# A gated cross-attention and quantised feed-forward block on one core: preparation and attention merged into one block of instructions, with the gate-weight jobs placed in attention steps

## The reference, cut to what matters

```python
def reference(x, ctx_1024, g_xattn, g_ffn, w_q, w_k, w_v, w_o, w_gate, w_up, w_down):
    # x is (4, 1024, 512), ctx_1024 is (4, 64, 512); 16 heads of 64
    x = x + jnp.tanh(g_xattn[0]) * xattn(_layernorm(x), ctx_1024, ctx_1024, w_q, w_k, w_v, w_o)
    x = x + jnp.tanh(g_ffn[0]) * ffn(_layernorm(x), w_gate, w_up, w_down)
    return x
# xattn: q, k, v projections, scores * 64**-0.5, causal mask (k_pos <= q_pos),
#        softmax over the 64 keys, weights @ v, @ w_o
# ffn:   x = act_qdq(x)                      (quantised by its largest absolute value)
#        up, gate = act_qdq(x @ lpbq_dequant(w_up).T), act_qdq(x @ lpbq_dequant(w_gate).T)
#        gate = act_qdq(gate * fixed_qdq_u16(sigmoid(gate)));  o = act_qdq(gate * up)
#        return o @ lpbq_dequant(w_down).T
# lpbq_dequant: per block of 32 weights, scale = max|w| / 7, round, times scale
```

## Time and profile before

| | us |
|---|---|
| median of 3 runs | 1515.85 (1515.39 to 1516.1) |
| the profiled execution | 1512.33 |
| its span | 1510.5 |
| PE busy | 1331.8 (88%) |
| DVE busy | 1097.1 (73%) |
| ACT busy | 596.8 (40%) |
| POOL busy | 241.3 (16%) |
| first instruction of attention (DVE) | at 71.09 |
| first chunk matmul of attention | at 79.50 |
| first matmul with gate weights (`gate_phase`) | at 586.32 |

### The profile page before, as it was taken

How to read it: one execution, slowest core, us unless ns; L and a number is a source line. 1 busy time by engine, 2 the same in 40 slices (tenths; PEclk the granted TensorE clock), 3 DMA queues, 4 the chain that set the end, 5 groups by cost and what they waited for, 6 DMA issues and landing times. The chain is left out here.

```text
span 1510.5 us, 18719 instructions
## 1 busy us (share of the span) xinstructions
PE 1331.8 (88%) x6141; PEld 1089.7 (72%) x6141; DVE 1097.1 (73%) x1460; ACT 596.8 (40%) x705; POOL 241.3 (16%) x249
## 2 busy tenths in 40 slices
PE   6589999999999985999999989999994009999999
PEld 5468877877886864788888868887883008888887
DVE  5557878878878853667777769998998995455453
ACT  2232232232223212334443335556667973333331
POOL 2112211212212210000100025551101000000000
PEclk9889999999999986999999989999997559999999
DMA  8701211211110117866665689996558863444443
GB/s 290 253 0 36 70 40 53 68 42 49 62 56 35 50 46 300 295 230 236 230 245 191 221 317 309 312 317 214 173 191 322 336 239 120 172 148 167 162 151 118
DMA packets 110998, 259.17 MB, mean 172 GB/s; under 512 B 10848, under 2 KB 23136, under 8 KB 109408
## 3 DMA queue, kind: packets, MB, share of 16 engines
q1 hardware_dynamic: 110656, 258.52, 49.0%
q10 hardware_dynamic: 288, 0.00, 0.0%
HBM read 151.52 MB, written 106.95 MB: 171 GB/s over the span
## 5 line engine op out<-in xcount | busy, mean ns | idle before, releaser
L1065 PE MATMUL gpG<-xph,Wh 128*128 128x512 f32 x384 | 153.1, 399 | 2.0 <-DVE xpl L985 2.0
L1539 PE MATMUL pD<-Wh,xph 128*128 128x512 f32 x384 | 150.3, 391 | 4.6 <-DVE xpl L1518 4.6
L1065 PE MATMUL pU<-xph,Wh 128*128 128x512 f32 x384 | 150.8, 393 | 0.7 <-POOLq L63 0.7
L1065 PE MATMUL gpG<-xph,Wl 128*128 128x512 f32 x384 | 150.7, 393 | 0.0
L1065 PE MATMUL gpG<-xpl,Wh 128*128 128x512 f32 x384 | 150.6, 392 | 0.0
L1065 PE MATMUL pU<-xpl,Wh 128*128 128x512 f32 x384 | 150.5, 392 | 0.0
L1065 PE MATMUL pU<-xph,Wl 128*128 128x512 f32 x384 | 150.3, 392 | 0.0
L1539 PE MATMUL pD<-Wl,xph 128*128 128x512 f32 x384 | 150.1, 391 | 0.0
L1539 PE MATMUL pD<-Wh,xpl 128*128 128x512 f32 x384 | 150.1, 391 | 0.0
L1518 DVE TENSOR_TENSOR xpl<-doq,xph 128x1536 fp32r<-128x1536 int16 (+1 forms) x34 | 56.4, 1664 | 122.8 <-ACT xph L1485 122.8
L968 ACT ACTIVATE gst<-gpG,sc 128x512 f32<-128x512 f32 x96 | 66.4, 692 | 170.3 <-PE gpG L1065 164.5
(11 more groups left out here) (169 smaller groups left out, 2912.6 us busy)
## 6 DMA issues: line engine op xcount, KB each, us to landing
dub<-up_d SPq DMA_DIRECT2D x42, 768.0 KB, 4.7
gate_d<-gst SPq DMA_DIRECT2D x96, 256.0 KB, 2.5
gb<-gate_d SPq DMA_DIRECT2D x32, 768.0 KB, 6.3
up_d<-ust SPq DMA_DIRECT2D x96, 256.0 KB, 4.4
xr<-xn_d SPq DMA_DIRECT2D x9, 1024.0 KB, 6.1
xph<-up_d SPq DMA_DIRECT2D x11, 768.0 KB, 6.0
xpl<-up_d SPq DMA_DIRECT2D x11, 768.0 KB, 6.1
xin<-in_x SPq DMA_DIRECT2D x32, 256.0 KB, 2.7
```

Of the source, the lines that this page charges most:

```text
L1065: mm = pe.matmul(ps[:, :], Ws[:, it, kt * P:(kt + 1) * P], xs[:, kt, :], start=(kt == 0 and Ws is Wh and xs is xh), stop=(kt == KT - 1 and ...
L1539: mm = pe.matmul(pD[4 * t + q][:, :], os_[n][:, cs], Ws[:, it, :], start=(it == 0 and os_ is oh and Ws is Wh), stop=(it == IT - 1 and os_ ...
```

## The change

`prepare` and `attend` become one function, `front_phase`, with one block and no barrier between. The edits:

1. The preparation keeps the projections and the turning of `wq`, in another order (all keys and `wq` first, then the values), and has no jobs. The first two tiles of x get their statistics and their normalisation within it.
2. The twelve jobs move into the attention loop: four per batch. Job q has its scale, divide and integer part in step q+3, and its turn, high and low part and its store in step q+4 (`job_at`). It uses the bank `pX` and two buffers.
3. Both normalisations move from DVE to ACT (`activation` with `Identity`, scale and bias). The bias is the negative mean times the reciprocal root, for which POOL's `rstd` gets two more instructions on one column: four where it had two.
4. On DVE the low part of x moves ahead of the integer part and of the maximum of the second normalisation.
5. In steps 0 and 8 PE transposes x behind the values and not ahead of them.
6. The spreading of the largest value goes by a transpose on PE and a maximum on DVE (`everywhere`) in place of `partition_all_reduce`.

```diff
+        JB = 4
+        J = Jobs(mk, ph, "pj", JB, 2, [pX])
...
+        def job_at(k, jobs, delay):
+
+            q = k - 3 - delay
+            return q if jobs and 0 <= q < JB else None
@@ SyncE @@
+            sp.dma_start(cx[:, :, :], cf.rearrange("(t p) d -> p t d", p=P)).then_inc(ctx_in, 16)
+            load(wk, w_k, wk_in, 0)
+            load(wq, w_q, wq_in, 0)
+            load(wk, w_k, wk_in, 1)
+            load(wq, w_q, wq_in, 1)
+            for j in range(2):
+                load_x(j)
+            for r in range(2):
+                load(wv, w_v, wv_in, r)
+            load_x(2)
+            sp.dma_start(wo[:, :, :], w_o.rearrange("(t p) n -> p t n", p=P)).then_inc(wo_in, 16)
+            for j in range(3, BQ):
+                load_x(j)
+            for q in range(2):
+                job_load(sp, J, 0, q, w_src[q, 0, :, :])
...
+                q = job_at(k, jobs, 1)
+                if q is not None:
+                    job_store(sp, J, b, q, job_dst(b, q))
+                    job_load(sp, J, b, q + J.NJ, job_src(b, q + J.NJ))
@@ GpSimd @@
+                pool.wait_ge(*at(eps_s, 3 * BQ * b, 3 * j + 2))
+                pool.tensor_tensor(rs_[:, n, 2:3], mv_[:, n, 0:1], rs_[:, n, 1:2], ALU.mult).then_inc(eps_s, 1)
+                pool.wait_ge(*at(eps_s, 3 * BQ * b, 3 * j + 3))
+                pool.tensor_tensor(rs_[:, n, 3:4], half[:, 2:3], rs_[:, n, 2:3], ALU.subtract).then_inc(rstd_s, 1)
...
                 if have(k - 3):
                     rstd(b, k - 3, mv2, rs2, mean2_done, eps2_done, rstd2_done, x2_done)
+                q = job_at(k, jobs, 0)
+                if q is not None:
+                    job_divide(pool, J, b, q)
                 if have(k - 1):
...
-            pool.wait_ge(sx_red, 1)
-            pool.partition_all_reduce(T1, T0, P, RMAX).then_inc(sx_all, 1)
@@ ScalarE @@
+            def normal(b, j, to, src, mv_, rs_, done):
+                n = j % 2
+                act.activation(to[n][:, :], src[:, :], ACT.Identity, bias=rs_[:, n, 3:4], scale=rs_[:, n, 1:2]).then_inc(done, 1)
...
                         act.activation(pTh[:, cs], pT[:, cs], ACT.Copy).then_inc(pTh_done, 1)
+                q = job_at(k, jobs, 1)
+                if q is not None:
+                    job_hi(act, J, b, q)
...
                 def high():
+                    if have(k + 2) and k + 2 >= 2:
+                        j = k + 2
+                        act.wait_ge(*tile(rstd_done, b, j))
+                        act.wait_ge(*tile(xT_ps, b, j - 2))
+                        normal(b, j, xn, xin[j % BQ], mv, rs, xn_done)
                     if have(k + 1):
...
                         act.activation(xh[j % 2][:, :], pX[:, :], ACT.Copy).then_inc(xh_done, 1)
+                    if have(k - 3):
+                        j = k - 3
+                        act.wait_ge(*tile(rstd2_done, b, j))
...
+                        normal(b, j, x2, x1[j % 2], mv2, rs2, x2_done)
@@ VectorE @@
                         dve.tensor_tensor(pTl[:, cs], pT[:, cs], pTh[:, cs].bitcast(F32), ALU.subtract).then_inc(pTl_done, 1)
+                q = job_at(k, jobs, 1)
+                if q is not None:
+                    job_lo(dve, J, b, q)
...
+                q = job_at(k, jobs, 0)
+                if q is not None:
+                    job_scale(dve, J, b, q)
                 if have(k - 1):
                     sums(b, k - 1)
-                some(2 if which == 0 else 1)
-                if have(k + 2):
-                    normal(b, k + 2)
-                some(1)
-                if have(k - 3):
-                    normal2(b, k - 3)
-                some(1)
+                some(2 if which == 0 else 3)
...
                     dve.tensor_tensor(xl[j % 2][:, :], pX[:, :], xh[j % 2][:, :].bitcast(F32), ALU.subtract).then_inc(xl_done, 1)
+                some(2)
+                if q is not None:
+                    job_integer(dve, J, b, q)
+                if have(k - 3):
+                    largest(b, k - 3)
                 some(8)
@@ TensorE @@
+                q = job_at(k, jobs, 1)
+                if q is not None:
+
+                    pe.wait_ge(*tile(xl_done, b, k))
+                    job_turn(pe, J, b, q, ident)
                 if have(k - 2):
                     j = k - 2
                     pe.wait_ge(*tile(prob_done, b, j))
...
+            for r in range(ROUNDS):
+                project(wk, r, wk_in, [(k_sb, r - 1)] if r >= 2 else [], k_ps)
...
+            for r in range(ROUNDS):
+                project(wv, r, wv_in, [(k_sb, 3 + r)] if r < 2 else [(v_sb, r - 1)], v_ps)
             schedule(pe, step)
-
+            pe.wait_ge(sx_red, 1)
+            everywhere(pe, pX[:, 0:P], T0, ident).then_inc(sx_spread, 1)
```

More of the change, by code:

```diff
@@ L128, in flamingo_block @@
          T0, T1, T2, T3, T4, AMAX, GPOS, GNEG, AP2, AN2) = [sc[:, n:n + 1] for n in range(25)]
[L130 to L143, removed]
+        front_phase(mk, xf, cf, (w_q, w_k, w_v, w_o), g_xattn, g_ffn, w_src[0], wsc[0], x1_d, xn_d, ident, mask, half, xmx,
+                    (TG_X, TG_F, RAW_X, RAW_F, S_X, INV_X, T0, T1))
+        release_sems()
         with ExitStack() as ff:
@@ L279, in by_input, with diagonal @@
     return [d[:, bass.ds(r * (3 * 512) + c * 512, 512)] for d in w]
[L282 to L291, removed]
+def diagonal(act, t, bd, b, done):
+    for a in range(2):
+        rows = slice(a * 64, a * 64 + 64)
+        act.activation(bd[rows, :, a * 64:a * 64 + 64], t[rows, :, bass.ds(CK * b, CK)], ACT.Copy).then_inc(done, 1)
@@ L471, in attend @@
+        vT = sb(ph, "vT", [P, PAIRS, B * CK], F32)
+        kbd = sb(ph, "kbd", [P, PAIRS, P], F32)
+        vbd = sb(ph, "vbd", [P, PAIRS, P], F32)
+        xin = [sb(ph, f"xin{n}", [P, H], F32) for n in range(BQ)]
         xn = [sb(ph, f"xn{n}", [P, H], F32) for n in range(2)]
@@ L826, in step, with turn_x @@
                             mm.then_inc(pT_ps, 1)
[L827 to L835 removed]
+                def turn_x():
+                    if have(k + 1):
+                        j = k + 1
+                        pe.wait_ge(*tile(xn_done, b, j))
+                        pe.wait_ge(*tile(xl_done, b, j - 1))
+                        if q is not None:
+                            pe.wait_ge(*at(J.lo_done, JB * b, q + 1))
+                        for kt in range(KT):
+                            mm = pe.transpose(pX[:, kt * P:(kt + 1) * P], xn[j % 2][:, kt * P:(kt + 1) * P], ident[:, :])
+                        mm.then_inc(xT_ps, 1)
@@ L836, in step @@
+                if which != 0:
+                    if have(k) and k >= 0:
+                        scores(b, k)
+                    turn_x()
                 values(b, k, have)
                 if which == 0:
+                    turn_x()
                     scores(b, k)
+            pe.wait_ge(id_set, 1)
+            pe.wait_ge(ctx_in, 16)
+            for kt in range(KT):
+                for t in range(2):
+                    mm = pe.transpose(pw[kt // 2][:, (kt % 2) * 256 + t * P:(kt % 2) * 256 + (t + 1) * P],
+                                      cx[:, t, kt * P:(kt + 1) * P], ident[:, :])
+                if kt % 2:
+                    mm.then_inc(ctxT_ps, 1)
@@ new lines, in _, with project @@
+            pe.wait_ge(ctxT_sb, 2)
+            def project(w, r, s_in, ready, s_ps):
+                pe.wait_ge(s_in[r // 2], 16)
+                for s, n in ready:
+                    pe.wait_ge(s, n)
+                for a in range(2):
+                    for kt in range(KT):
+                        mm = pe.matmul((pk, pv)[r % 2][:, a * 256:(a + 1) * 256], w[:, kt, (2 * r + a) * P:(2 * r + a + 1) * P],
+                                       cT[:, kt, :], start=(kt == 0), stop=(kt == KT - 1))
+                mm.then_inc(s_ps, 1)
```

350 lines of the change are left out of this document (133 added, 217 removed).

## The result

The changed kernel takes 1536.82 us (1534.06 to 1541.29, 4 runs) against 1515.97 for the kernel before beside it: ratio 1.0146, interval 1.0127 to 1.0165. It is 20.9 us slower, where +8.5 was predicted. Its profiled execution took 1541.29, span 1539.5; it is the longest of the four, 4.5 above the median, so sums over two profiles come out some 8 us larger than the difference of the medians.

What follows compares the result with a forecast made beforehand. No one engine bounds preparation; TensorE bounds plain attention steps. Terms from -35.6 (preparation) to +40 (jobs) sum to +8.5 on profiled 1512.33, giving 1520.8; with 3.5 for the median, 1524.5. Own range 1518 to 1532, wide 1503 to 1535.

Steps and rivals of the forecast that it cites:

- Preparation: Projections and transposes before attention: the first chunk of attention comes at 43.9 instead of 79.50, -35.6 us.
- First chunk steps: From 79.30 to 113.90, clock loss after the pause goes away: -2 us (0 to -2.4).
- Plain steps of batch 3: Three steps without a job: GpSimd's extra short instructions exceed its slack, 0.15 a step, +0.5 us (0 to +1).
- Jobs in attention steps: Attention steps with jobs: divide, held integer instruction, product and turn delay TensorE, 13.35 a batch, +40 us (+22 to +50).
- Chunk steps: Loop's chunk steps: x transposes behind the values, +1.2 us; ScalarE's normalisations ahead of the second step's high part, +7.5.
- the direct 2.8: Second chunk step: first high part, behind two normalisations on ScalarE, at 222.1 where 219.27 stood, +2.8 us.
- End: End of attention: spreading the maximum takes 0.93 where 4.64 is spent, the last root is 0.54 longer, -3.1 us.
- the clock falls: Rival, chance 0.10: job steps make TensorE wait 2.9, turn and transposes run at half clock, +12, 1536 us.
- nothing is held: Rival, chance 0.20: in job steps integer and product run beside GpSimd's multiplication, 22 us in all, time 1506.
- the swap is even: Rival, chance 0.12: GpSimd's short instructions string tighter, a job step costs 2.7, a second chunk step 2.2, time 1516.
- Preparation stays long: Rival, chance 0.06: a late load or slow clock makes preparation end at 50 and not 43.9, time 1531.
- VectorE relief: Rival, chance 0.04: moving normalisations off VectorE shrinks the chunk steps by 2 each, total -12, time 1504.

## Why the prediction was wrong, point by point

The direction was right. The kernel's time lies 1.8 us above the wide range, 1503 to 1535, and 4.8 above the forecast's own, 1518 to 1532. (The sum itself gives 1512.33 + 8.5 + 3.5 = 1524.3, where 1524.5 is written.) By its own steps:

- **Preparation, -35.6**: measured -35.69. Right, and the transfers kept up.
- **First chunk steps, -2**: wrong. From the first chunk to step 3 it is 47.10 before and 47.03 after. The clock did rise from 0.93 to 1.00, and TensorE's busy time fell by 1.7 (42.37 to 40.67), but its idle time grew by as much: the waits for the low parts of the first chunks went from 0.8 to 2.8.
- **Plain steps of batch 3, +0.5**: 72.74 against 72.78, so nothing in all. The mechanism is there all the same: steps 4 and 5 are 12.42 with GpSimd's four short instructions and 12.29 without them, 0.13 as forecast. The kernel before had steps of 12.43 and 12.39 in its batch 3 too, and a last one that was 0.2 longer.
- **Jobs in attention steps, +40**: the jobs cost 46.8. Of that 7.5 is the stall at the jump, which no step and no rival had. The remaining 39.3 is the predicted mechanism: held integer, product, turn. That it is so near 40 is in part luck. It is counted from the kernel without jobs, whose steps 3 to 7 are together already 1.5 a batch longer than the 12.29 each that the prediction counted from, 4.5 us in all, and it holds 3 to 7 us of clock that I had left to a rival.
- **Chunk steps, +8.7**: without the jobs they cost 3 x 0.5 and 3 x 3.25 = 11.3. The second was sized at 2.5, the value "near the direct 2.8". Of the 3.25, 2.4 is more idle time and 0.9 is TensorE's longer busy time (21.18 against 20.28), at a clock of 0.93 against 1.00: the loss by the clock, which the prediction had named at 1.6, was not won back in full.
- **End, -3.1**: from the transposes of the last tile to the first gate matmul it is 33.67 before and 31.04 after, -2.6. The spread itself gave 3.75. The other 1.1 was lost beside it; the longer last root and ScalarE's 0.81 stand there, but what each costs was not measured.

The step that failed is the term of the jobs: it priced what stands in a step and left out what the added instructions do to the loop that holds them. They took VectorE's body from 255 to 261 instructions in the built program, and with that body VectorE is idle for 5.2 us at each of two jumps back, 3.6 of which TensorE sees. Of the 12.3 us by which the forecast was too low, this is 7.5, shown by writing out the loop and by padding the body of a kernel without jobs. Against the jobless kernel, the other parts of the change gained 26.7 where the prediction had 31.5 (-35.6 - 2 + 0.5 + 8.7 - 3.1); that is the other 5. The spans of the two profiles differ by 22.9 only, so the traces show 8.6 and not 5: in the chunk steps (2.6 more), in step 5 of the loop (2.7), in the loop's other steps (1.5), in the first chunks (1.7), in 0.6 at the end, against 0.5 less in the last batch.

The rival "the clock falls" had named 1536, almost the measured time, for a cause that is worth 3 to 7 us in the job steps: that the number fits is luck. The rival "nothing is held" is refuted by the 2.11 against 0.39 for one instruction, and "the swap is even" by job steps of 15.5, where it had 15.0. "Preparation stays long" and "VectorE relief" did not happen.

Two things stay open: why the first chunk step is 22.2 in some turns of the loop and 23.7 in others, and whether the stall comes with the length of the body (then somewhere between 255 and 261) or with where its end falls.

## What to carry to other kernels

A piece of work that is spread over the steps of a full engine costs its chain of hand-overs, not its work: look for the place where each part's input has been ready for long, one step later if need be, and put it *behind* what the full engine waits for in every other queue. Here the same jobs fell from 47 us to 15 (1504.8 against 1490.0) by that and by writing out the loop. When instructions are added to a loop, count the body on each engine, look for idle time put down to "issue" at its first instruction, and compare the packets of the instruction queue. And when an in-order engine takes over work, ask what it had been doing first for the busiest engine: one chunk copied ahead of the normalisations was worth 10 us. Last, a total that agrees with a rival's number is no sign for the rival: here 1536 stood beside 1536.8 for another cause.

## What the runs showed of the hardware

- A jump back on VectorE with a body of 261 or 263 instructions leaves it idle 5.2 to 5.7 us; with 255 or 223 it is idle 0.8 to 1.6, all of which is a wait for ScalarE. 128 instructions ahead of the loop make no difference. Four instruction packets lie around each of these jumps, and none with 255; 39 against 28 in the whole kernel.
- The integer instruction on VectorE, 128x512 from SBUF to SBUF, takes 0.39 to 0.40 away from GpSimd's multiplication and 1.89 to 2.11 when that multiplication, 1.90 long, has started 0.07 to 0.30 before it; it ends 0.27 to 0.30 behind that one.
- ScalarE with a bias and a scale for each partition, 128x512 from SBUF, takes 0.80 to 0.82; its copies of the same size from PSUM take 0.57 to 0.61.
- TensorE's granted clock was 0.93 over the first batch's job steps with waits of 1.88 to 2.54 us, and 1.00 with the waits filled, or at 1.44 to 1.50. Where the chain of other engines bounds the step, this difference was worth 3 to 7 us in a kernel of 1537. Over the second chunk step it was 0.93 with a wait of 3.02 and 1.00 with one of 1.43, and TensorE's busy time there 21.14 and 19.52.
